# Query and key strips of an attention stage brought from 16 and 17 rows to 32

## The chip, the cores and the metric

The kernel runs on one core of a Trainium2 chip. The metric is the device time of one execution, in microseconds (us), lower is better. The engines are called as the profile calls them: PE is the matrix engine (TensorE), PEld its weight loads, DVE the vector engine, ACT the scalar engine, POOL GpSimd, SP the engine that only issues transfers here.

## The reference

The whole program is a chain of six blocks on an image batch of shape (8, 64, 32, 32): twelve layers of a state space model, a convolution block with attention, the image attention that is changed here, a graph attention with experts, a slice attention and a block of 16 experts. All is float32. The block that the change touches is this, per image (T = 1024 tokens, 64 channels, 4 heads of 16):

```python
Wh = (h @ W).reshape(B, T, 4, 16).transpose(0, 2, 1, 3)
scores = jnp.einsum('bhtd,bhsd->bhts', Wh, Wh) * 0.25
attention = softmax(leaky_relu(scores, negative_slope=0.2), axis=-1)
h_prime = jnp.einsum('bhts,bhsd->bhtd', attention, Wh)
```

Query and key are the same tensor. `h` is the layer-normed stream, and `h_prime` is added to it.

## The kernel before

The stages of the program run one after the other, each in a block of its own with its own semaphores. The stage in question is `graph_attn_stage` (L962). It works on 16 sets, one for each pair of heads of each of 8 images. A set has 16 slots: the 1024 query tokens in two halves of 512, times 8 blocks of 128 keys. The engines' queues are made from one list of slots, from -32 to 260, and each engine takes the slots in that order. A set's scores come in slots 0 to 15 of it; what prepares a set is spread over the slots of the sets before.

The identity leaky_relu(s) = max(s, 0.2 s) is used with exponentials: exp of the larger is the larger exp. So there are two branches, s and 0.2 s, each with its own strip of rows. `key` and `query` are tiles of 128 partitions that hold four strips of 32 partitions, for two heads times two branches (`head_rows`, L1047). In a strip, rows 0 to 15 are the head's 16 channels. Row 16 holds 1 in `key` and, in `query`, minus the query's largest possible exponent, so that a product over 17 rows gives the exponent already shifted. Rows 17 to 31 hold zeros: the weights `ws` that make the strips are padded with zero columns (an input prepared so), and ACT's bias `K_UNIT` is 1 on row 16 of each strip alone.

In one slot:

- `scores` (L1078): PE makes, for each of two heads, two products of 17 rows by 128 keys by 512 queries, one for each branch, into `g_ab` (one PSUM tile for each head). Each product is two instructions in the trace (float32). The products of head h wait until ACT has read head h's tile of the slot before (`exped`).
- `exps` (L1162): ACT takes the exponential of both branches of a head at once, 1024 columns, into `g_both`; `larger` (L1212): DVE takes the larger of the two branches for both heads.
- `sums` (L1093), every second slot: PE multiplies with the values, 128 rows by 32 columns, four at once into four column strips of `g_sum`; `keep_sum` copies it out at every fourth of these.
- `maxima` (L1107), for a coming set: PE multiplies 16 rows of `key` (128 of its tokens) with 16 rows of `key` (all 1024 tokens, in two strips) into `g_top`, of which DVE takes the row's maximum (L1224). A new product waits for the reading of the one before (`top_read`). It is placed after the slot's scores in PE's queue, so the next slot's scores stand behind it.
- `side` (L1121, and ACT's part L1177): single steps of a set, which share the PSUM tile `g_side`: `turn` and `values` once an image, `heads0` and `heads1` two sets ahead (PE makes half a tile, ACT writes `key` with the bias, then `query` with the scale and releases `g_side`), `rows` one set ahead, at slot 13 (the 16 columns of negated maxima are turned into rows; SP sends them to DRAM and back in four transfers to row 16 of each strip of `query`, and the set's first scores wait for `rows_in`), and `out` at slot 3 of the next set (the sums are turned back, DVE divides and adds).

POOL gathers for a later stage in the first slots of this one, and DVE goes on with that stage's search after its last slot.

Of the kernel before, what the change touches and what calls it, by code (L numbers as in the profile page):

```python
# [2 lines left out]
P = 128  # L3
B, C, H, W = 8, 64, 32, 32
L = H * W
# [953 lines left out]
HEADS2, HDIM2 = 4, 16  # L959


def graph_attn_stage(nc, w_strips, w_plain, consts, m_rows, tn_sb, t_sb, search):  # L962
# [9 lines left out]
    ALU, ACT, AX = mybir.AluOpType, mybir.ActivationFunctionType, mybir.AxisListType.X  # L972
# [41 lines left out]
    with ExitStack() as ctx:  # L1014
        def sb(name, shape, dt=fp32):
            return ctx.enter_context(nc.sbuf_tensor(name, shape, dt))
# [10 lines left out]
        tnT = [sb(f"g_tnT{k}", [C, L]) for k in range(2)]  # L1027
        val = [sb(f"g_val{k}", [P, PER, HEADS2, 32]) for k in range(2)]
        key, query = ([sb(f"g_{n}{k}", [P, L]) for k in range(3)] for n in ("key", "query"))
        both = [sb(f"g_both{k}", [P, 2, 2, HALF]) for k in range(2)]  # L1030
        E = [sb(f"g_E{k}", [P, 2, HALF]) for k in range(4)]
        oT = [sb(f"g_oT{k}", [P, HALF]) for k in range(2)]
# [11 lines left out]
        rows_out, rows_in = sem("g_rows_out"), sem("g_rows_in")  # L1044
        halves = [slice(0, HALF), slice(HALF, L)]

        def head_rows(h, branch, rows=HDIM2 + 1):  # L1047
            at = 32 * (2 * h + branch)
            return slice(at, at + rows)

        with nc.Block() as block:
            @block.sync
# [21 lines left out]
            @block.tensor  # L1074
            def _(pe):
                M = nc.tensor.matmul

                def scores(g):  # L1078

                    p, s = slot_of(g)  # L1080
                    half, j = divmod(s, PER)
                    if s == 0:
                        pe.wait_ge(rows_in, p * 64 + 64)
                    for h in range(2):
                        if g:
                            pe.wait_ge(exped, 2 * (g - 1) + h + 1)
                        for branch in range(2):
                            rows = head_rows(h, branch)
                            last = M(pair_ps[h][:, halves[branch]], key[p % 3][rows, j * P:(j + 1) * P],  # L1089
                                     query[p % 3][rows, halves[half]], start=True, stop=True)  # L1090
                        last.then_inc(scored, 1)

                def sums(r):  # L1093

                    pe.wait_ge(maxed, 2 * r + 2)
                    if r and r % 4 == 0:
                        pe.wait_ge(sum_kept, r // 4)
                    for g in (2 * r, 2 * r + 1):
                        p, s = slot_of(g)
                        j = s % PER  # L1100
                        for h in range(2):
                            at = 32 * (2 * (j % 2) + h)
                            last = M(sum_ps[at:at + 32, :], val[p // 2 % 2][:, j, p % 2 * 2 + h, :], E[g % 4][:, h, :],
                                     start=j < 2, stop=j >= PER - 2)
                    last.then_inc(summed, 1)

                def maxima(p, b):  # L1107

                    h, i = divmod(b, PER)
                    n = maxima_no[p, b]  # L1110
                    if b == 0:
                        pe.wait_ge(side_read, event_no["heads1", p] + 1)
                    if n:
                        pe.wait_ge(top_read, n)
                    for half in range(2):
                        rows = head_rows(h, half, HDIM2)
                        last = M(top_ps[:, halves[half]], key[p % 3][rows, i * P:(i + 1) * P], key[p % 3][rows, halves[half]],  # L1117
                                 start=True, stop=True)
                    last.then_inc(topped, 1)

                def side(kind, at):  # L1121

                    n = event_no[kind, at]
                    if n:
                        pe.wait_ge(side_read, n)
                    if kind.startswith("turn"):
                        first = at * PER + 4 * int(kind[-1])
                        for i in range(4):
                            last = M(side_ps[0:C, i * P:(i + 1) * P], tn_sb[:, first + i, :], con[:, K_ID:K_ID + P],
                                     start=True, stop=True)  # L1130
                    elif kind == "values":
                        for i in BLK:
                            last = M(side_ps[:, i * C:(i + 1) * C], tnT[at % 2][:, i * P:(i + 1) * P], wq[:, :], start=True, stop=True)
                    elif kind.startswith("heads"):
                        last = M(side_ps[:, :], ws[:, at % 2, :], tnT[at // 2 % 2][:, halves[int(kind[-1])]], start=True, stop=True)
                    elif kind == "rows":
                        pe.wait_ge(negated, at + 1)
                        last = M(side_ps[0:SLOTS, 0:P], negm[:, :], con[:, K_ID:K_ID + P], start=True, stop=True)
                    else:
                        pe.wait_ge(sum_kept, 2 * at + 2)  # L1140
                        for i in BLK:
                            last = M(side_ps[:, i * C:(i + 1) * C], oT[i // 4][:, i % 4 * P:(i % 4 + 1) * P], fold[:, :],
                                     start=True, stop=True)
                    last.then_inc(side_made, 1)

                pe.wait_ge(loaded, 48)
                pe.wait_ge(folded, 1)
                for g in slots:
                    if 0 <= g < ALL:
                        scores(g)  # L1150
                    if sum_at(g) is not None:
                        sums(sum_at(g))
                    if event_at(g):
                        side(*event_at(g))
                    if maxima_at(g):
                        maxima(*maxima_at(g))

            @block.scalar
            def _(act):
                A = nc.scalar.activation  # L1160

                def exps(g):  # L1162
                    for h in range(2):
                        act.wait_ge(scored, 2 * g + h + 1)
                        if g >= 2:
                            act.wait_ge(maxed, g - 1)
                        A(both[g % 2][:, h, :, :].rearrange("p a t -> p (a t)"), pair_ps[h][:, :], ACT.Exp).then_inc(exped, 1)  # L1167

                def keep_sum(r):

                    half = r // 4
                    act.wait_ge(summed, r + 1)
                    if half >= 2:
                        act.wait_ge(side_made, event_no["out", half // 2 - 1] + 1)
                    A(oT[half % 2][:, :], sum_ps[:, :], ACT.Copy).then_inc(sum_kept, 1)

                def side(kind, at):  # L1177
                    if kind == "out":
                        return
                    act.wait_ge(side_made, event_no[kind, at] + 1)  # L1180
                    if kind.startswith("turn"):
                        done = A(tnT[at % 2][:, halves[int(kind[-1])]], side_ps[0:C, :], ACT.Copy)
                    elif kind == "values":
                        act.wait_ge(ones_set, 2)
                        if at >= 2:
                            act.wait_ge(summed, (at - 1) * SLOTS)
                        done = A(val[at % 2][:, :, :, 0:HDIM2], side_ps[:, :].rearrange("p (i h d) -> p i h d", i=PER, h=HEADS2), ACT.Copy)
                    elif kind.startswith("heads"):
                        hs = halves[int(kind[-1])]
                        A(key[at % 3][:, hs], side_ps[:, :], ACT.Identity, bias=con[:, K_UNIT:K_UNIT + 1])  # L1190
                        done = A(query[at % 3][:, hs], side_ps[:, :], ACT.Copy, scale=con[:, K_UNIT + 1:K_UNIT + 2])
                    else:
                        if at:
                            act.wait_ge(rows_out, at * 16)
                        done = A(mT[:, :], side_ps[0:SLOTS, 0:P], ACT.Copy)
                    done.then_inc(side_read, 1)

                nc.scalar.preload_act_table_set("natural_log_exp_and_others")
                act.wait_ge(loaded, 48)
                for g in slots:  # L1200
                    if 0 <= g < ALL:
                        exps(g)
                    if sum_at(g) is not None and sum_at(g) % 4 == 3:
                        keep_sum(sum_at(g))
                    if event_at(g):
                        side(*event_at(g))
# [1701 lines left out]
```

## Time and profile before

| | |
|---|---|
| time, median of 3 runs | 12822.3 us (12805.16 to 12825.92) |
| profiled execution, own time | 12828.42 us |
| its span, first to last instruction | 12826.2 us |
| PE busy | 7784.8 us (61%) |
| DVE busy | 7413.5 us (58%) |
| POOL busy | 7085.3 us (55%) |
| ACT busy | 4851.3 us (38%) |
| mean granted TensorE clock | 0.746 of full speed |

The busy times are sums over stages that have different limits; the stage of the change is 12% of the span, from 7052 us to 8535 us. The granted clock is 1.00 for 2.4 GHz and 0.50 for 1.2 GHz, and a value between the two for a stretch is a mixture of both levels. The profiled execution was 6.1 us longer than the median of the runs, and 2.2 us of its time lie outside its span.

### The profile page before, as it was taken

Reading aid. Unit: us, or ns where it says so; the run is one execution under the profiler, and the core shown is the slowest. Engines: PE = TensorE matmul, PEld = TensorE weight load, DVE = VectorE, ACT = ScalarE, POOL = GpSimd, SP = SyncE. Lnnn points to the kernel's source line nnn. Section 1 sums busy time; section 2 is a strip of 40 time slices with the busy share of each in tenths; the row PEclk is TensorE's granted clock in tenths of the full one; section 3 lists DMA queues with packets and bytes.
Section 4 is the critical chain, followed back from the end, with each engine's and each line's share of the span. In section 5 each row is a group of like instructions: output and inputs, shape, how many; then the busy total and the mean of one; then the engine's idle time right before and its main releaser. Section 6 shows DMA issues by size and latency. Waiting matters only on the chain. (4 is left out here: it accounts for less than half of the span.)

```text
span 12826.2 us, 85840 instructions
## 1 busy us (share of the span) xinstructions
PE 7784.8 (61%) x22295; PEld 3300.0 (26%) x22295; DVE 7413.5 (58%) x5674; ACT 4851.3 (38%) x5239; POOL 7085.3 (55%) x4572
## 2 busy tenths in 40 slices
PE   0288888888888888887787799970000000000469
PEld 0133333333333333332343233330000000000342
DVE  8599999999999999998222344431111111110424
ACT  0166666666666666664011244430111111110124
POOL 0088888888888888887100100006666666666017
PEclk8599999999999999999666555555555555555569
DMA  0155555555555555555000000003222222221012
GB/s 8 39 154 155 155 155 155 153 156 154 155 155 155 153 155 156 154 156 142 4 0 0 8 1 1 1 2 34 16 16 16 16 16 16 17 17 11 3 38 89
DMA packets 387922, 959.19 MB, mean 75 GB/s; under 512 B 124066, under 2 KB 159458, under 8 KB 385442
## 3 DMA queue, kind: packets, MB, share of 16 engines
q1 hardware_dynamic: 302786, 930.45, 26.5%
q0 software_dynamic: 75808, 26.27, 4.7%
q10 hardware_dynamic: 9216, 1.05, 0.1%
q8 instruction: 61, 1.00, 0.0%
q14 instruction: 51, 0.42, 0.0%
HBM read 905.13 MB, written 50.89 MB: 75 GB/s over the span
## 5 line engine op out<-in xcount | busy, mean ns | idle before, releaser
L502 POOL TENSOR_TENSOR hC<-h,Cb 128x1024 f32<-128x1024 f32 x1536 | 3611.6, 2359 | 935.8 <-DVE h L581 934.8
L581 DVE TENSOR_TENSOR_SCAN h<-dA,B_ps 128x1024 f32<-128x1024 f32 x1536 | 3512.4, 2287 | 68.1
L285 PE MATMUL y_ps<-hC,con 128*128 128x512 f32 x6144 | 2910.4, 595 | 92.9 <-DVE gz L587 56.9
L432 ACT ACTIVATE dA<-delta,negA 128x1024 f32<-128x1024 f32 x1536 | 1765.8, 1150 | 1831.8 <-DVE h L581 1831.2
L2357 POOL DMA_INDIRECT g_got<-scratch_node,g_idx x2048 | 1951.8, 953 | 898.9 <-issue 898.7
L573 DVE TENSOR_TENSOR B_ps<-dx,B_ps 128x1024 f32<-128x1024 f32 x1536 | 1855.2, 1208 | 94.7 <-PE B_ps L279 94.7
L2373 PE MATMUL g_ps_y<-g_wout,g_hid 128*128 128x64 f32 x512 | 126.0, 428 | 2544.8 <-ACT g_hid L2413 1496.5
L285 PEld LDWEIGHTS y_ps<-hC,con 128*128 128x128 f32 x6144 | 1136.8, 189 | 1128.3 <-issue 740.5
L279 PE MATMUL B_ps<-Bpart,sel 96*128 96x512 bf16 x3072 | 925.7, 383 | 675.1 <-DVE h L581 674.0
L2443 DVE TENSOR_TENSOR g_e<-g_tgt,g_got 128x128 f32<-128x128 f32 x64 | 27.1, 424 | 2057.7 <-DMA g_got<-scratch_node,g_idx 2057.7
L2397 ACT ACTIVATE g_w_ps<-g_w 128x128 f32<-128x128 f32 x64 | 18.0, 282 | 2237.0 <-issue 901.5
L1089 PE MATMUL g_ab<-g_query,g_key 17*128 17x512 f32 x2048 | 846.5, 1091 | 10.0 <-ACT g_both L1167 10.0
L2247 POOL MEMSET r_ad<- 128x4 f32 x1 | 0.1, 102 | 1524.9 <-POOLq L1295 1524.9
L2373 PEld LDWEIGHTS g_ps_y<-g_wout,g_hid 128*128 128x128 f32 x512 | 113.9, 327 | 2645.4 <-ACT g_hid L2413 1556.2
L1224 DVE TENSOR_REDUCE g_mrow<-g_top 128x1 f32<-128x1024 f32 x256 | 313.6, 1225 | 789.1 <-PE g_top L1117 720.1
L1167 ACT ACTIVATE g_both<-g_ab 128x1024 f32<-128x1024 f32 x512 | 508.8, 1023 | 672.6 <-PE g_ab L1089 672.6
L279 PEld LDWEIGHTS B_ps<-Bpart,sel 96*128 96x128 bf16 x3072 | 234.2, 98 | 1670.4 <-DVE h L581 1407.2
L1117 PE MATMUL g_top<-g_key 16*128 16x512 f32 x1024 | 514.2, 1101 | 62.2 <-issue 39.8
L1071 POOL MEMSET g_val<- 128x1024 f32 x2 | 1.8, 950 | 913.3 <-POOLq L931 913.3
L1544 POOL TENSOR_TENSOR eb_scaled<-eb_above,eb_share 64x1024 f32<-64x1024 f32 x128 | 301.6, 2356 | 125.1 <-PE eb_ps L1498 76.7
L1089 PEld LDWEIGHTS g_ab<-g_query,g_key 17*128 17x128 f32 x2048 | 286.9, 312 | 287.5 <-issue 154.3
L1217 DVE TENSOR_TENSOR g_E<-g_both 128x1024 f32<-128x1024 f32 x256 | 311.3, 1216 | 51.6 <-ACT g_both L1167 51.4
(477 smaller groups left out, 10931.7 us busy)
## 6 DMA issues: line engine op xcount, KB each, us to landing
Cb<-scratch_c_rows SPq DMA_DIRECT2D x3072, 256.0 KB, 3.9
g_got<-scratch_node,g_idx POOLq DMA_INDIRECT x2048
eb_share<-scratch_gate_rows SPq DMA_DIRECT2D x128, 256.0 KB, 3.5
scratch_edge<-g_out SPq DMA_DIRECT2D x64, 384.0 KB
par<-in_ssm SPq DMA_DIRECT2D x48, 395.5 KB, 4.8
scratch_c_rows<-Crow SPq DMA_DIRECT2D x96, 128.0 KB, 3.7
scratch_place<-s_zero SPq DMA_DIRECT2D x4, 1024.0 KB, 8.6
g_tgt<-scratch_place SPq DMA_DIRECT2D x1, 4096.0 KB
```

The lines of the kernel that those rows point to most:

```text
L279: last = nc.tensor.matmul(B_ps[k % 2][:, hs], sel[:, n, :], Bpart[d][:, hs], start=True, stop=True)
L285: last = nc.tensor.matmul(y_ps[:, hs], con[:, K_ID:K_ID + P], hC[k % DEEP][:, hs], start=(k == 0), stop=(k == STEPS - 1))
L432: A(dA[k % DEEP][:, :], delta[d][:, :], ACT.Exp, scale=negA[:, n:n + 1]).then_inc(decay_ready, 1)
L502: G.tensor_tensor(hC[k % DEEP][:, :], hst[k % DEEP][:, :], Cb[k % DEEP][:, :], ALU.mult).then_inc(prod_ready, 1)
L573: V.tensor_tensor(B_ps[k % 2][:, :], dx[dir_of(k)[0]][:, :], B_ps[k % 2][:, :], ALU.mult).then_inc(dbu_ready, 1)
L581: V.tensor_tensor_scan(hst[k % DEEP][:, ::step], dA[k % DEEP][:, ::step], B_ps[k % 2][:, ::step], 0.0, ALU.mult, ALU.add).then_inc(scanned, 1)
L1089: last = M(pair_ps[h][:, halves[branch]], key[p % 3][rows, j * P:(j + 1) * P], query[p % 3][rows, halves[half]], start=True, stop=True)
L1117: last = M(top_ps[:, halves[half]], key[p % 3][rows, i * P:(i + 1) * P], key[p % 3][rows, halves[half]], start=True, stop=True)
L1167: A(both[g % 2][:, h, :, :].rearrange("p a t -> p (a t)"), pair_ps[h][:, :], ACT.Exp).then_inc(exped, 1)
L1217: V.tensor_tensor(E[g % 4][:, :, :], both[g % 2][:, :, 0, :], both[g % 2][:, :, 1, :], ALU.max).then_inc(maxed, 1)
L1224: V.reduce_max(mrow[:, b:b + 1], top_ps[:, :], AX).then_inc(top_read, 1)
L2357: nc.gpsimd.indirect_dma_start(out=got[k][:, j, :], out_offset=None, in_=node_tbl, in_offset=Off(ap=idx[k][:, j:j + 1], axis=0)).then_inc( ...
```

## The change

All products of the strips are taken over 32 rows, where the scores had 17 and the maxima 16. For the scores this adds rows that hold zeros on both sides. For the maxima it takes in row 16, which is 1 in `key`; so that it adds nothing, the moving operand is no longer `key` but `plain`, a new tile (two buffers) that ACT fills with the heads as they are, with row 16 zero. That is one more ACT instruction of 128x512 in each `heads` step, between the two that were there. Nothing else is moved.

```diff
+        plain = [sb(f"g_plain{k}", [P, L]) for k in range(2)]
...
-        def head_rows(h, branch, rows=HDIM2 + 1):
+        def head_rows(h, branch):
             at = 32 * (2 * h + branch)
-            return slice(at, at + rows)
+            return slice(at, at + 32)
...
-                        rows = head_rows(h, half, HDIM2)
-                        last = M(top_ps[:, halves[half]], key[p % 3][rows, i * P:(i + 1) * P], key[p % 3][rows, halves[half]],
+                        rows = head_rows(h, half)
+                        last = M(top_ps[:, halves[half]], key[p % 3][rows, i * P:(i + 1) * P], plain[p % 2][rows, halves[half]],
                                  start=True, stop=True)
...
                         A(key[at % 3][:, hs], side_ps[:, :], ACT.Identity, bias=con[:, K_UNIT:K_UNIT + 1])
+                        A(plain[at % 2][:, hs], side_ps[:, :], ACT.Copy)
                         done = A(query[at % 3][:, hs], side_ps[:, :], ACT.Copy, scale=con[:, K_UNIT + 1:K_UNIT + 2])
```

## Rows read from the trace of the kernel before

**Rows 1.** Busy time by stretch: us, busy of PE, PEld, DVE, ACT, POOL, then granted clock.
```profile
3000.00:3400.00 400.00, 337.68 (x881) 137.29 (x881) 391.64 (x232) 255.02 (x253) 331.65 (x146) 1.00 0.57 156
6617.00:6634.00 17.00, 17.00 (x21) 6.64 (x20) 6.53 (x6) 0.00 (x0) 0.00 (x0) 0.50 0.00 0
6678.20:6688.40 10.20, 10.20 (x25) 3.31 (x24) 0.00 (x0) 0.00 (x0) 0.00 (x0) 1.00 0.00 0
6800.00:7000.00 200.00, 180.43 (x366) 80.41 (x367) 49.79 (x47) 24.65 (x27) 0.00 (x0) 0.67 0.00 0
7177.00:8525.00 1348.00, 1328.27 (x4558) 463.49 (x4562) 599.92 (x568) 578.16 (x634) 0.00 (x0) 0.51 0.00 1
12500.00:12700.00 200.00, 200.00 (x828) 61.24 (x824) 95.52 (x140) 83.14 (x140) 158.90 (x69) 1.00 0.29 89
7203.60:7207.00 3.40, 3.40 (x20) 1.90 (x16) 0.07 (x1) 0.67 (x2) 0.00 (x0) 0.50 0.00 0
7207.00:7210.40 3.40, 3.40 (x27) 2.17 (x23) 2.36 (x2) 2.31 (x3) 0.00 (x0) 1.00 0.00 0
7210.40:7213.80 3.40, 3.40 (x15) 1.49 (x14) 0.86 (x1) 1.40 (x2) 0.00 (x0) 0.50 0.03 5
```

**Rows 2.** PE's instructions in order of time, in stretches of Rows 1: start, length.
```profile
6622.28 3.62 PE L751 MATMUL psA<-k_sb,q_sb 32*128 32x512 f32 x4
...
6672.57 16.60 PE L769 MATMUL psM<-E,vT 128*65 128x512 f32 x32 [2.41 <-ACT E L831]
...
12599.90 0.59 PE L1497 MATMUL eb_ps<-tnT_b,eb_w 64*128 64x512 f32 x1
12599.91 0.59 PE L1498 MATMUL eb_ps<-eb_scaled,eb_w 64*128 64x512 f32 x1
```

**Rows 3.** PE's instructions in order of time, around the stage's first rise of the clock.
```profile
7202.90 1.94 PE L1103 MATMUL g_sum<-g_E,g_val 128*32 128x512 f32 x8
7204.77 1.97 PE L1129 MATMUL g_side<-g_con,tn_a 128*64 128x128 f32 x8
...
7207.36 1.45 PE L1089 MATMUL g_ab<-g_query,g_key 17*128 17x512 f32 x6
7208.74 2.15 PE L1133 MATMUL g_side<-g_w,g_tnT 64*128 64x64 f32 x16
```

**Rows 4.** PE's instructions in order of time, two slots of the stage at clock 0.50.
```profile
7438.86 1.94 PE L1103 MATMUL g_sum<-g_E,g_val 128*32 128x512 f32 x8
...
7440.75 1.22 PE L1089 MATMUL g_ab<-g_query,g_key 17*128 17x512 f32 x2
...
7441.76 2.74 PE L1089 MATMUL g_ab<-g_query,g_key 17*128 17x512 f32 x6
...
7446.00 2.62 PE L1089 MATMUL g_ab<-g_query,g_key 17*128 17x512 f32 x8
7448.55 1.94 PE L1103 MATMUL g_sum<-g_E,g_val 128*32 128x512 f32 x8
```

**Rows 5.** Groups of the stretch 7177 to 8525: busy, mean ns, idle before and its end.
```profile
L1167 ACT ACTIVATE g_both<-g_ab 128x1024 f32<-128x1024 f32 x511 | 507.8, 1023 | 672.6 <-PE g_ab L1089 672.6
L1217 DVE TENSOR_TENSOR g_E<-g_both 128x1024 f32<-128x1024 f32 x255 | 310.1, 1216 | 49.6 <-ACT g_both L1167 49.5
L1224 DVE TENSOR_REDUCE g_mrow<-g_top 128x1 f32<-128x1024 f32 x238 | 291.5, 1225 | 695.0 <-PE g_top L1117 694.8
```

**Rows 6.** All engines in order of time, the last slots, which hold no maxima.
```profile
8486.82 2.09 PE L1089 MATMUL g_ab<-g_query,g_key 17*128 17x512 f32 x8
...
8494.81 2.09 PE L1089 MATMUL g_ab<-g_query,g_key 17*128 17x512 f32 x8
```

**Rows 7.** The same view of the start, and of one set's maxima on their way.
```profile
7072.43 0.69 ACT L1190 ACTIVATE g_key<-g_side,g_con 128x512 f32<-128x512 f32 x1 [2.16 <-issue]
7073.01 0.68 ACT L1191 ACTIVATE g_query<-g_side,g_con 128x512 f32<-128x512 f32 x1
...
7423.14 1.10 SPq L1064 DMA_DIRECT2D g_query<-scratch_m_rows  x4
```

## The prediction, made before the changed kernel was run

> **What bounds the kernel now.** I read busy time by stretch first. The stage's main part, 7177 to 8525 us, is 1348.0 us long; PE is busy in 1328.3 us of it, DVE in 600, ACT in 578, POOL in nothing [rows 1]. The groups say the same from the other side: ACT's exponentials stood idle 672.6 us for PE's scores, DVE's maxima 694.8 us for PE's products, and what was waited for the other way round is small [rows 5]. So PE sets the pace, 1348.0 / 256 = 5.27 us a slot.
>
> The same rows hold the peculiar thing: PE is 98.5% busy and its granted clock is 0.51, that is 1.2 GHz almost throughout. A busy PE has either level in this trace, and what differs is how many of the array's 128 rows the instructions fill:
> - one strip of 32 rows at a time (L751), PE 100% busy: clock 0.50 [rows 1, 2];
> - 128 rows (L769), PE 100% busy: 1.00 [rows 1, 2];
> - two strips of 64 rows side by side (L1497 and L1498 start 0.01 us apart): 1.00, for 200 us on end [rows 1, 2];
> - 84% busy, with products of 96 and 128 rows (the twelve layers): 1.00 [rows 1];
> - here: the stretch before the clock rose at 7207 held nothing but the sums and a turning of tokens, both of 128 rows; in the stretch after it came strips of 17 rows and products of 64 rows, and the clock went back to 0.50, with PE busy all the time [rows 1, 3]. The trace has five such rises in the stage.
>
> The turning has a unit matrix as its moving operand, nearly all zeros, and the clock rose after it all the same [rows 3]. So I read: what counts is rows taken part in, not their values, nor busy time.
>
> **The order of two slots, at the low clock.** From one sum to the next are 7448.55 - 7438.86 = 9.69 us [rows 4]. The sum takes 1.87 us of it (start to next start, 7438.86 to some 7440.73). The rest is nine passes: a pass over 512 columns is (2.74 - 0.20) / 3 = 0.85 us, six passes lie between 7440.75 and 7446.00 and three between 7446.00 and 7448.55 [rows 4]. Maxima of one pair of strips run beside scores of the other pair, so it comes to nine passes where one after the other would be twelve. 4.85 us a slot, then; the other 0.42 are the side steps.
>
> **What the change adds.** (a) Rows: 17 and 16 become 32. Does a pass get longer? The four passes of 32 rows at L751 took 3.62 us from first start to last end, 0.85 each and a tail of 0.2, as the 17-row passes do [rows 2, 4]. Cost nothing. The Trainium skill (TensorE: Matmul & The Clock Gate, LDWEIGHTS) says that weight loads go by columns and that the row count doesn't matter; by this too the sum stays as it is.
> (b) One ACT copy in each of 32 heads steps. ACT's second pass there starts 7073.01 - 7072.43 = 0.58 us after the first [rows 7]; I price the third alike. Four of them lie before the stage's first slots, two on the path of the first set (1.2 us). The other 28 lie among ACT's work, 28 x 0.58 = 16 us; ACT has 2.3 us of work a slot (578.2 / 256 [rows 1]), so at the old pace they hide in 3 us of idle time a slot. At a faster pace some delay the next exponential: I charge half, 8 us. Bounds: nothing, and 32 x 0.68 = 22 us.
> (c) `g_side` is released 0.58 us later; the next side step is at least a slot away, and the next set's maxima wait for `heads1` only four slots on. Nothing. SP's row transfers are untouched: four issues of 1.10 us together make up its last part [rows 7]. The chain has three slots until the set's first scores, 15.8 us now and some 10 at the pace below; at an estimated 5 us, the issues four times over, it stays hidden. `plain` has two buffers, and its last reader is more than a set behind when it is written again, so no wait is added.
>
> **What the change gives.** The mean number of rows at work, at the old pace: scores 2048 passes x 17 rows x 0.85 us, maxima 960 x 16 x 0.85, the sums 128 rows for 256 passes x 0.85, over 1348 us, with some 7 from side steps: 22 + 10 + 21 + 7 = 60 of 128. With 32 rows: 41 + 19 + 21 + 7 = 88. A slot of both heads' scores at once fills the array as the two 64-row strips do [rows 2], and scores beside maxima of the other pair fill it too. So dense stretches come in nearly every slot and the clock should rise soon after the first scores. Once it is high, a pass takes (1.45 - 0.16) / 3 = 0.43 us [rows 3].
>
> How long is a slot at the high clock? From below, PE's own work: two slots are 9 x 0.43 + 0.17 (change to whole rows) + a sum of 1.02 = 5.06, so 2.53; the side steps' 0.42 shrink to 0.6 of it (a choice: a half if all were streams, more where weight loads set the time), 0.25: 2.8 us. ACT (2.3 + 0.1) and DVE (1.216 + 1.225 + some 0.1 [rows 5]) come to 2.4 and 2.5, so neither is beyond this. From above, the chain of waits: in the last slots, without maxima, two slots take 8494.81 - 8486.82 = 7.99 us, though PE has little to do: scores, exponential, scores, exponential, sum in a row by the queues' order [rows 6]. Three of its pieces are PE streams of 1.71 us that halve: 7.99 - 2.56 = 5.43. Two maxima that overlap nothing add 1.9, the side steps 0.5: 7.8 for two, 3.9 a slot. In the middle of the stage part of the maxima overlap scores, as in the nine passes above; I take the mean of the bounds, 3.35 us.
>
> How much of the stage is at the high clock? Then waits appear on PE, and 64-column steps whose time is weight loads, so it will fall now and again and stay low for a while. The stage before this one, which goes back and forth between strips of 32 rows and products of 128, had 0.67 as a mean, so a third of its time at the high level; the twelve layers have 1.00 with 84% busy [rows 1]. At the high pace the rows at work are still 88 x 5.27 / (2 x 3.35) = 69 of 128. That is nearer the layers than the stage before, whose low half is one strip of 32. I take 0.80 of the time; the bounds are 0.34 and 1.00 by these two rows, and with so many more rows I call 0.55 the likeliest case's lower end.
>
> **The sum.** Slots per us: 0.80 / 3.35 + 0.20 / 5.27 = 0.277; 256 slots take 925 us in place of 1348: -423. Copies +9. Net -414. The start (its maxima wait for DVE and for transfers) and the stages around it are unchanged. Against the profiled execution: 12828.4 - 414 = 12414, span 12412. That execution was 6.1 us over the median, so the runs should come to 12822.3 - 414 = 12408.
>
> **Rivals.**
> 1. The clock doesn't move, because a started strip already counts as 32 rows, or zeros don't count, or busy time is what counts. Then only the copies are left: 12822 + 1 = 12823. For it: I infer the rule from some ten stretches. Against: four strips of 17 rows come often here and the stage stayed at 0.51, where two strips of 64 held 1.00 [rows 1, 2]. The Trainium skill (TensorE: Matmul & The Clock Gate, Part 1) has the clock go by how busy the engine has been; by that rule PE at 98.5% would be at 1.00 before, and padding would change nothing. The rows differ from it: 0.51. 10%.
> 2. It rises but falls back at once, since at 2.4 GHz the same work leaves PE waiting: 0.30 of the time high. 0.30 / 3.35 + 0.70 / 5.27 = 0.222 a us, 1151 us, -197 + 9: 12634. This is about the lower bound of a third. For it: each of the five rises ended at once (one of them in [rows 1]). Against: those came with 17 rows. 7%.
> 3. Faster still, high throughout and better overlapped than I allow: 256 x 3.1 = 794, -554 + 9: 12277. 4%.
> 4. Slower: the clock stays low and the new ACT copy falls on the path twice, since exponentials and the release of `g_side` both come later. 2 x 0.68 x 32 = 44 us: 12866. It decides from 0.80 us a step (26 us in all). Against: ACT's 673 us of waiting for PE [rows 5]. 2%.
>
> **How the numbers follow.** The forecast has 77%: 12408. Its own range: at 3.35 us and always high, 256 x 3.35 = 858, gives 12341; 0.55 at 3.9 gives 0.55 / 3.9 + 0.45 / 5.27 = 0.226, 1131 us, 12614. The whole range, 12310 to 12640, takes in rival 2's middle and leaves out rivals 1 and 4 and most of 3, with a little of the tails. What a measurement of this kernel can tell from no change is 0.2%, 26 us. Faster: forecast, rivals 2 and 3, 88%. Same: rival 1, 10%. Slower: 2%.
>
> **What would show it.** In the changed profile, the granted clock of the stage should be near 0.9 (0.5 + 0.5 x 0.8) and a slot 3.6 us, with most scores' passes 0.43 us apart; ACT's idle time for scores should fall from 673 us to some 300. PE should no longer be busy nearly all the time. 32 more ACT instructions of 0.68 us. If the clock reads 0.51 the rows' theory is wrong; if it reads 0.9 and a slot is above 4 us, the chain of waits was underpriced; if SP's transfers end PE's waits at every 16th slot, (c) was.

## The result, and the profile after

The changed kernel takes 12299.68 us (median of 4 runs, 12287.58 to 12304.47) where the kernel before, now run more often, takes 12813.73 us. The ratio is 0.9598, 95% interval 0.9581 to 0.9614: 4.0% faster, some 514 us. I had forecast 12408 with a range from 12310 to 12640. The direction and the mechanism were right; the gain was a quarter larger than the 414 us of the forecast, and the time lies 10 us below the range. Of those 10 us the starting point has a part: I had counted from 12822.3 us for the kernel before, and its median is now 8.6 us lower.

The page of the changed kernel, part 2: 40 slices of the span, busy tenths of PE and granted clock in tenths.

```profile
PE   0188888888888888888688779920000000000569
...
PEclk8599999999999999999866689955555555555569
```

Counted from 0, the slices 23 to 25, where the stage lies, have a clock of 5 each before and of 8, 9 and 9 now. Busy time by stretch of the changed kernel, columns as in [rows 1]; the first row shown is the stage from its first exponential to its last, the other three are a stretch just before a fall of the clock, the one after it, and the one in which it has risen again:

```profile
7167.50:7996.20 828.70, 764.33 (x4550) 290.00 (x4548) 598.42 (x567) 569.23 (x663) 0.00 (x0) 0.98 0.01 1
...
7493.90:7496.50 2.60, 0.40 (x2) 0.00 (x0) 2.54 (x4) 1.94 (x2) 0.00 (x0) 1.00 0.00 0
7497.20:7500.60 3.40, 3.40 (x16) 1.48 (x14) 0.58 (x1) 1.19 (x2) 0.00 (x0) 0.50 0.00 0
7500.60:7504.00 3.40, 3.40 (x28) 1.51 (x26) 1.77 (x2) 2.05 (x3) 0.00 (x0) 1.00 0.00 0
```

(The dots stand for rows of other stretches.) Before, the stage had 1348.0 us [rows 1], some 3 of them ahead of its first exponential; it has become 516 us shorter, 1345.1 to 828.7 when both are counted from the first exponential. The medians differ by 514 us and the two profiled spans (12826.2 and 12294.8) by 531, so this stage holds nearly all of the gain. Of the other 15 us of the spans' difference 14 lie ahead of it, 8 before the convolution block's first product of queries and keys and 6 from there to the stage's first step, in code that the change doesn't touch; they are a difference between two executions. DVE and ACT are busy 598 and 569 us, in substance as before. PE does the same passes in 764 us of busy time in place of 1325. The granted clock is 0.98, where it was 0.51: 2.4 GHz in place of 1.2.

The groups of the stage in the changed kernel, columns as in [rows 5]:

```profile
L1168 ACT ACTIVATE g_both<-g_ab 128x1024 f32<-128x1024 f32 x512 | 496.8, 1023 | 246.3 <-PE g_ab L1090 245.6 <-DVE g_E L1219 0.7
L1090 PE MATMUL g_ab<-g_query,g_key 32*128 32x512 f32 x2040 | 464.5, 630 | 9.0 <-ACT g_both L1168 9.0
...
L1226 DVE TENSOR_REDUCE g_mrow<-g_top 128x1 f32<-128x1024 f32 x236 | 288.9, 1224 | 199.9 <-PE g_top L1118 191.6
L1118 PE MATMUL g_top<-g_plain,g_key 32*128 32x512 f32 x944 | 271.8, 652 | 41.9 <-DVE g_mrow L1226 41.9
```

ACT's idle time for scores fell from 672.6 to 245.6 us and DVE's for maxima from 694.8 to 191.6 [rows 5]. They are the same instructions with the same means, 1023 and some 1224 ns; what is gone is waiting for PE. PE's instructions in order of time, two slots of the changed kernel, against [rows 4]:

```profile
7415.52 1.07 PE L1104 MATMUL g_sum<-g_E,g_val 128*32 128x512 f32 x8
7416.52 0.70 PE L1118 MATMUL g_top<-g_plain,g_key 32*128 32x512 f32 x2
7416.53 0.70 PE L1090 MATMUL g_ab<-g_query,g_key 32*128 32x512 f32 x2
...
7417.06 1.44 PE L1090 MATMUL g_ab<-g_query,g_key 32*128 32x512 f32 x6
7419.06 1.13 PE L1118 MATMUL g_top<-g_plain,g_key 32*128 32x512 f32 x4 [0.56 <-DVE g_mrow L1226]
```

Three passes that took 2.74 us take 1.44, the sum 1.07 in place of 1.94. And something is new: an idle time of PE in brackets, in which it waits for DVE to have read the last maxima. Before, it came to 1.4 us in the whole stage; now it is 41.9.

### The profile page after: what moved, and what is told of

It is laid out like the page before. It is cut to its first block and busy times, and to the rows that moved or that the text cites. A ratio compares the mean times of both kernels' runs of the same rounds, so it can differ in the third digit from the quotient of the medians.

```text
span 12294.8 us, 85872 instructions
## 1 busy us (share of the span) xinstructions
PE 7209.1 (59%) x22295; PEld 3122.8 (25%) x22295; DVE 7412.1 (60%) x5674; ACT 4837.6 (39%) x5271; POOL 7077.4 (58%) x4572
## 5 line engine op out<-in xcount | busy, mean ns | idle before, releaser
L1168 ACT ACTIVATE g_both<-g_ab 128x1024 f32<-128x1024 f32 x512 | 496.8, 1023 | 246.3 <-PE g_ab L1090 245.6
L1226 DVE TENSOR_REDUCE g_mrow<-g_top 128x1 f32<-128x1024 f32 x256 | 313.4, 1224 | 299.1 <-PE g_top L1118 218.6
L1090 PE MATMUL g_ab<-g_query,g_key 32*128 32x512 f32 x2048 | 468.3, 631 | 9.0 <-ACT g_both L1168 9.0
L1118 PE MATMUL g_top<-g_plain,g_key 32*128 32x512 f32 x1024 | 313.3, 690 | 103.0 <-DVE g_mrow L1226 60.3
```

What stands on the lines that cost most here:

```text
L1226: V.reduce_max(mrow[:, b:b + 1], top_ps[:, :], AX).then_inc(top_read, 1)
```

## The experiments

Theory 1, that of the prediction: PE's granted clock follows the rows that its instructions take part in. The rivals: it follows busy time alone; only full strips count; values count; or the gain has another cause (the new operand). Each kernel ran against the kernel before on the same chip, and the ratios are to it. Clock and length of the stage are rows of the view by stretch, from its first exponential to the end of its last larger-of-two, in one trace of each kernel.

| kernel | ratio (95%) | median, us | stage, us | clock |
|---|---|---|---|---|
| kernel before | 1 | 12800 to 12814 | 1345.1 | 0.51 |
| changed kernel | 0.9598 (0.9581 to 0.9614) | 12299.7 | 828.7 | 0.98 |
| copies only | 1.0001 (0.9991 to 1.0010) | 12801.3 | 1332.2 | 0.51 |
| maxima on 32 rows | 0.9915 (0.9898 to 0.9931) | 12689.2 | 1188.6 | 0.60 |
| both on 24 rows | 0.9843 (0.9826 to 0.9859) | 12601.0 | 1157.5 | 0.64 |
| scores on 32 rows | 0.9665 (0.9649 to 0.9681) | 12371.9 | 934.0 | 0.84 |
| both on 28 rows | 0.9652 (0.9636 to 0.9668) | 12358.4 | 900.0 | 0.88 |
| ones in the padding | 0.9610 (0.9594 to 0.9626) | 12315.7 | 828.6 | 0.98 |
| copy twice | 0.9639 (0.9623 to 0.9655) | 12347.4 | 861.3 | 0.96 |
| maxima first | 0.9603 (0.9587 to 0.9619) | 12309.4 | 829.5 | 0.95 |
| turning later | 0.9608 (0.9590 to 0.9625) | 12301.5 | 828.2 | 0.97 |
| copies on POOL | 0.9620 (0.9603 to 0.9638) | 12312.6 | 833.7 | 0.96 |
| convolution strips too | 0.9478 (0.9462 to 0.9493) | 12150.7 | 828.3 | 0.98 |
| all together | 0.9459 (0.9442 to 0.9476) | 12110.0 | 805.2 | 0.98 |

### One part of the change alone

Only the copy and the new operand, rows as before:

```diff
+        plain = [sb(f"g_plain{k}", [P, L]) for k in range(2)]
...
-                        last = M(top_ps[:, halves[half]], key[p % 3][rows, i * P:(i + 1) * P], key[p % 3][rows, halves[half]],
+                        last = M(top_ps[:, halves[half]], key[p % 3][rows, i * P:(i + 1) * P], plain[p % 2][rows, halves[half]],
...
+                        A(plain[at % 2][:, hs], side_ps[:, :], ACT.Copy)
```

> Only the new ACT copy and the new moving operand of the maxima; scores stay at 17 rows, maxima at 16. Theory 1, the rows that PE's instructions take part in set its granted clock: the clock stays at 0.51 in the stage, the time is that of the kernel before plus 1 to 22 us (the copies), some 12815 to 12835. Rival, the new operand is what helped (key is no longer read as weights and as moving operand at once): the stage is short as in the changed kernel, some 12300.

The rival falls: ratio 1.0001, clock 0.51. The time, 12801.3 us, lies below the 12815 to 12835 that I had named, but the kernel before took 12800.4 us beside it. The copies cost nothing that can be measured at the low clock; ACT waits for PE 652 us there. The stage is 13 us shorter in this trace than in that of the kernel before: it holds some 38 us at the high clock where the other has 17. Such short rises come in both, and with one trace of each I read no effect from it.

Only the scores on 32 rows (`rows=32` as the default of `head_rows`, the maxima as before, no copy):

> Only the scores go to 32 rows, maxima stay at 16 rows of key, no copy. Mean rows at work at the old pace 79 of 128, against 60 before and 88 with both. Theory 1 (rows count as they are): the clock is high for most of the stage, over 0.85 as a mean, time 12300 to 12450. Rival, only a stretch whose strips are all full counts: the maxima, in nearly every slot, break it, clock below 0.65, time over 12600.

Only the maxima on 32 rows (with the copy, scores on 17):

> Only the maxima go to 32 rows, with the copy; scores stay at 17. Mean rows at work at the old pace 69 of 128. Theory 1: between the two kernels, the clock goes up and down, 0.55 to 0.85 as a mean, time 12450 to 12780. Rival (only full strips count): the clock stays at 0.51, time 12815 to 12835.

Both times came out within theory 1's numbers, 12371.9 and 12689.2 us, and so did the second clock, 0.60; the first, 0.84, was just below the 0.85 that was named. Full strips aren't needed everywhere for the clock to rise: with the maxima at 16 rows in nearly every slot the clock was 0.84, high for two thirds of the stage. The two parts give 3.35% and 0.85%, together 4.2%; measured together they give 4.0%.

### The same instructions with fewer rows

```diff
-            return slice(at, at + 32)
+            return slice(at, at + 24)
```

and the same with 28.

> Scores and maxima both on 24 rows, with the copy: the same instructions as in the changed kernel, fewer rows. Mean rows at work at the old pace 73 of 128. Theory 1: between the two kernels, nearer the changed one, clock 0.65 to 0.95 as a mean, time 12320 to 12650. Rival (only full strips count): 0.51 and 12815 to 12835. Rival (a strip counts once it has more than 16 rows, so that the scores were never the matter): as changed, 12300.

> Scores and maxima both on 28 rows, with the copy. Mean rows at work at the old pace 36 + 17 + 21 + 7 = 81 of 128, about the 79 that the kernel with only its scores on 32 rows has. If it is the rows at work that set the clock, however they come together, the two should be alike: clock of the stage 0.80 to 0.93, time 12330 to 12420. Rival, full strips are what matters (32 or nothing): like the 24-row kernel or below, clock under 0.65, time over 12600.

24 rows: 12601.0 us, within the range that was named, but nearer to the kernel before than to the changed one, where I had expected the opposite; the clock, 0.64, was just below what I had named. 28 rows: 12358.4 us at 0.88, beside 12371.9 us at 0.84 for the kernel whose scores alone have 32 rows. Counted as in the prediction, the first has 36 + 17 + 21 + 7 = 81 rows at work at the old pace and the second 41 + 10 + 21 + 7 = 79. Two different edits with nearly the same rows have nearly the same time. That is the strongest evidence for rows: PE's instructions have the same count, order and columns in all these kernels. What it doesn't separate is rows from rows times columns: every product whose rows were changed has 128 columns. Full columns aren't needed, at least: products of 128 rows and 65 columns had the clock at 1.00 [rows 1, 2]. The stage by stretch, one row from each kernel. Copies only:

```profile
7175.50:8507.70 1332.20, 1311.57 (x4550) 454.28 (x4548) 598.70 (x566) 592.24 (x663) 0.00 (x0) 0.51 0.00 1
```

Both on 24 rows:

```profile
7171.00:8328.50 1157.50, 1118.51 (x4552) 398.27 (x4550) 598.62 (x566) 583.08 (x663) 0.00 (x0) 0.64 0.00 1
```

Both on 28 rows:

```profile
7169.10:8069.10 900.00, 839.43 (x4550) 317.71 (x4548) 598.65 (x566) 570.27 (x663) 0.00 (x0) 0.88 0.00 1
```

In the first PE is busy 98.5% of the time and has the low clock; in the third it is busy 93% and has mostly the high one. So a high busy share isn't enough for the high clock, and a somewhat lower one doesn't prevent it. Busy time does matter where there is little of it: in the 40 slices above, the changed kernel's slices 27 to 36 have PE at 0 tenths and the clock at 5.

### What the padding holds

```diff
-    k[:, K_UNIT] = row % 32 == HDIM2
+    k[:, K_UNIT] = row % 32 >= HDIM2
```

> The changed kernel with rows 17 to 31 of each key strip holding 1 in place of 0 (the query rows there stay 0, so the products are the same). Theory 1 (rows taken part in, whatever they hold): same as the changed kernel, 12290 to 12310, clock of the stage 0.98. Rival, values matter to the clock or to the time: different from it by more than 0.3%.

Ratio 0.9610 against 0.9598, intervals overlapping (the median, 12315.7 us, is 6 us above what theory 1 named, and the ratios differ by 0.12%, less than the rival's 0.3%), the stage 828.6 us and the clock 0.98 to the digit. With zeros or ones in `key`'s padding rows it is the same. The other side, `query`'s rows, stayed zero in both, so data that are nonzero on both sides weren't tried.

### The price of the copy at the high clock

```diff
                         A(plain[at % 2][:, hs], side_ps[:, :], ACT.Copy)
+                        A(spare[at % 2][:, hs], side_ps[:, :], ACT.Copy)
```

> The changed kernel with a second ACT copy of the heads in each heads step, into a tile that nobody reads: prices the added copy at the high clock. By my prediction's term (half of 0.58 us on the path, 32 times) +9 us on the changed kernel, 12300 to 12315. Rival, the copies are on the path in full at the high clock: +19 us or more. Rival, hidden: 0.

By medians it takes 48 us more, so the +9 of theory 1 was wrong and the rival's +19 or more came true. The stage took 861.3 us, 32.6 more than the changed kernel's 828.7, at a clock of 0.96: more than the 16 us that 28 copies last, start to next start. The clock has a part in it. In the 15 sets from the first to the last of the sets' turned maxima (`g_mT`), which take 27.5 us more (815.7 and 788.2), the low clock lasts some 58 us where the changed kernel has 26. At 5.27 us a slot low and 3.19 high (worked out further down), by an estimate from these rows, those 32 us cost 13; what is left, 15, is about the full length of the 28 copies.

The other way round, 28 of the 32 copies on POOL (PE's wait for them is left out here):

```diff
+                        nc.gpsimd.tensor_scalar(plain[at % 2][:, hs], key[at % 3][:, hs], con[:, K_UNIT:K_UNIT + 1], None,
+                                                ALU.subtract).then_inc(plain_made, 1)
...
-                        A(plain[at % 2][:, hs], side_ps[:, :], ACT.Copy)
+                        if at < 2:
+                            A(plain[at % 2][:, hs], side_ps[:, :], ACT.Copy)
```

> The changed kernel with 28 of the 32 added copies taken from ACT and made on the idle POOL, from the key tile (minus the unit row). The doubled copy cost the full 0.58 us each on the path at the high clock and let the clock fall longer. By that, taking 28 away gives -16 us or a little more, 12270 to 12290. Rival, the first copy was hidden and only the second was not: 0. Rival, POOL and DVE get in each other's way or the maxima now wait for POOL: 0 to +20.

No gain: 12312.6 us, the stage 833.7. The 15 sets took 783.8 us where the changed kernel took 788.2 (before: 1281.9). That difference is small but can be read: three traces whose stage has the same instructions, those of the changed kernel, of the one with ones in the padding and of the one with the convolution strips below, have 788.2, 788.3 and 787.8. The last slots, with the clock at 0.75 where the changed kernel has 0.93, took 9.5 us longer and more than gave it back. So taking 28 first copies away is worth some 4 us in those 15 sets, and adding 28 second ones costs 27.5. The price isn't in proportion even without the clock's part, and whether POOL's 1562 ns for such a copy hides a part of the gain I can't tell apart.

### What makes the clock fall, and what a slot waits for

In the middle of the changed kernel's stage the clock falls five times (at 7285.6, 7497.2, 7603.0, 7708.8 and 7814.6 us), each time at the turning of the next image's tokens. PE has been idle for 2.23 us before it, waiting for DVE. There are six such waits, 13.4 us in all; the one at 7392 us was followed by no fall. Two more falls are in the last slots. The wait at 7392, by stretch:

```profile
7390.00:7394.00 4.00, 1.91 (x16) 1.35 (x18) 2.43 (x5) 2.44 (x3) 0.00 (x0) 1.00 0.00 0
7394.00:7398.00 4.00, 4.00 (x32) 1.70 (x28) 2.36 (x2) 2.53 (x3) 0.00 (x0) 1.00 0.01 4
```

The one before the fall at 7497, all engines in order of time (the dots leave out weight loads, the maxima's products and some steps of DVE and ACT):

```profile
7494.63 1.21 DVE L1219 TENSOR_TENSOR g_E<-g_both 128x1024 f32<-128x1024 f32 x1
7495.77 0.25 DVE L1248 RECIPROCAL g_rden<-g_side 128x16 f32<-128x16 f32 x1
7496.05 0.42 DVE L1249 TENSOR_TENSOR g_tmp<-g_side,g_rden 128x256 f32<-128x256 f32 x1
...
7496.53 1.36 PE L1130 MATMUL g_side<-g_con,tn_a 128*64 128x128 f32 x8 [2.23 <-DVE g_tmp L1249]
...
7497.84 1.22 PE L1090 MATMUL g_ab<-g_query,g_key 32*128 32x512 f32 x2
...
7498.85 1.06 PE L1090 MATMUL g_ab<-g_query,g_key 32*128 32x512 f32 x2
```

The turning needs `g_side`, which DVE reads for the set before; DVE has its larger-of-two first in its queue. The next passes, 1.06 us in place of 0.59, are at the low clock. One slot more between the two steps takes the wait away:

```diff
-        if s in (4, 5) and p % 2 == 0 and p // 2 + 1 < B:
-            return f"turn{s - 4}", p // 2 + 1
-        if s == 6 and p % 2 == 0 and p // 2 + 1 < B:
+        if s in (5, 6) and p % 2 == 0 and p // 2 + 1 < B:
+            return f"turn{s - 5}", p // 2 + 1
+        if s == 7 and p % 2 == 0 and p // 2 + 1 < B:
```

> The changed kernel with the turning of the next image's tokens and its values one slot later (slots 5, 6, 7 in place of 4, 5, 6). In the profile after, PE stands idle 2.2 us before each turning, for DVE's last step of the set before, and the clock falls right after each of the seven. If this idle time is what makes it fall: no fall but at the stage's ends, clock of the stage over 0.99, -10 to -25 us on the changed kernel (12275 to 12290). Rival, it is the sparse products of the turning and of the output that make it fall: seven falls as before, time within 10 us of the changed kernel or only the idle 7 x 2.2 = 15 us less.

By stretch, all of the stage but its last slots, and the last slots; first the kernel with the turning later, then the changed kernel:

```profile
7177.00:7940.00 763.00, 717.49 (x4328) 274.65 (x4326) 576.35 (x547) 532.29 (x625) 0.00 (x0) 1.00 0.01 1
7940.00:8006.00 66.00, 56.36 (x230) 15.94 (x224) 22.69 (x21) 35.95 (x38) 0.00 (x0) 0.66 0.00 1
```
```profile
7177.00:7940.00 763.00, 707.74 (x4262) 272.22 (x4256) 565.02 (x536) 522.38 (x615) 0.00 (x0) 0.99 0.01 1
7940.00:7996.00 56.00, 47.01 (x254) 14.04 (x250) 26.80 (x26) 39.87 (x43) 0.00 (x0) 0.94 0.00 1
```

Half of the expectation came true (it counts seven falls, where five of six waits had one). None of PE's waits for `g_tmp` and no fall is left before the last slots, so the falls came with the idle time, not with the steps: the turning is there, one slot later, and the output products are unchanged. The 15 sets take 772.8 us, -15.4. But the last slots, which have no maxima, run at a clock of 0.66 where the changed kernel had 0.94. The two lower rows begin at the same time, when this kernel was already 5 us further on; from the last turned maxima to the stage's end it takes 66.8 us in place of 51.8, 15 us more. The sum is nothing: 0.9608.

```diff
+                    if maxima_at(g):
+                        maxima(*maxima_at(g))
                     if sum_at(g) is not None:
                         sums(sum_at(g))
                     if event_at(g):
                         side(*event_at(g))
-                    if maxima_at(g):
-                        maxima(*maxima_at(g))
```

> The changed kernel with PE's maxima of a slot placed before its sums and side steps, not after them. If a slot at the high clock is set by DVE waiting for the maxima and PE waiting for DVE's reading (the profile after shows 219 us of DVE waiting for maxima and 60 us of PE for DVE), DVE gets its work earlier and a slot falls from 3.24 to some 3.0 us, time 12220 to 12280. If PE's own stream sets it, or the next slot's scores come no earlier, no change: 12290 to 12310.

No gain as a whole, 0.9603. The 15 sets took 779.2 us, 9 less than in the changed kernel, in spite of a clock that was low for longer: some 58 us of these sets in place of 26. By the estimate above that costs 13 us, so the new order was worth some 22, and the clock took more than half of it back. The falls are at other places here than the turning: the first four of them come right after PE has been idle 0.83 us for an exponential, in the slots behind a `heads` step. Whether that idle time brings them no run tests. The last slots took 6 us more.

### The same idea in the stage before

In the convolution block's attention, products of one strip of 32 rows go one after another [rows 2]. Here there is nothing to put beside them, so each image's queries were laid in a tile of 128 partitions with zeros in the other 96, the keys of both images in one with zeros in its last 64 partitions, and the product taken over 128 rows:

```diff
-        q_sb, k_sb = sb("q_sb", [Q_COLS, L]), sb("k_sb", [Q_COLS, L])
+        q_sb, k_sb = [sb(f"q_sb{k}", [P, L]) for k in range(2)], sb("k_sb", [P, L])
...
+                for t in (*q_sb, k_sb):
+                    nc.gpsimd.memset(t[:, :], 0.0).then_inc(zeroed, 1)
...
-                        qb, kb = q_sb[32 * b:32 * b + 32, :], k_sb[32 * b:32 * b + 32, :]
+                        qb, kb = q_sb[b], k_sb
...
-                    A(q_sb[:, :], psM[0:Q_COLS, :], ACT.Identity, bias=cw[0:Q_COLS, CV_BQ:CV_BQ + 1]).then_inc(act_done, 1)
+                    for b in IMAGES:
+                        rows = slice(32 * b, 32 * b + 32)
+                        last = A(q_sb[b][rows, :], psM[rows, :], ACT.Identity, bias=cw[rows, CV_BQ:CV_BQ + 1])
+                    last.then_inc(act_done, 1)
...
```

> The changed kernel, and in the stage before it (convolution block with attention) the same idea carried further: its products of one strip of 32 rows, PE 100% busy at clock 0.50, are taken over 128 rows, with zeros in all others (query of each image in a tile of its own, one more ACT pass an image pair). Theory 1: these 384 passes of 0.85 us go to 0.43 us, and the clock of that stage from 0.67 to over 0.85; -130 to -200 us, 12100 to 12170. Rival (only packing of strips side by side raises the clock, or zero rows on the moving side don't count as here both operands' other rows are almost all zeros): clock unchanged, time 12300 to 12310.

12150.7 us, ratio 0.9478 against 0.9598: 149 us less than the changed kernel by medians, within the expectation; the clock of the stretch, 0.84, is just below the 0.85 that was named. Most of that stage by stretch, in the changed kernel:

```profile
6160.00:6960.00 800.00, 712.41 (x1563) 333.91 (x1563) 197.53 (x194) 93.35 (x98) 0.00 (x0) 0.65 0.00 0
```

and in this one:

```profile
6160.00:6800.00 640.00, 549.11 (x1534) 288.03 (x1533) 193.21 (x191) 92.83 (x97) 0.00 (x0) 0.84 0.00 0
```

PE's instructions of this kernel in order of time, as the clock rises:

```profile
6404.29 3.78 PE L753 MATMUL psA<-k_sb,q_sb 128*128 128x512 f32 x4
6407.86 2.95 PE L753 MATMUL psB<-k_sb,q_sb 128*128 128x512 f32 x4
6410.65 1.88 PE L753 MATMUL psA<-k_sb,q_sb 128*128 128x512 f32 x4
```

The same work (197.5 and 193.2 us of DVE, 93.4 and 92.8 of ACT) in 640 us where it took 800. Four passes take 3.78 us at first, about as they did over 32 rows (3.62 [rows 2]), and then 1.88. 96 of the 128 rows add nothing but zeros to an image's product, and the clock rises with them all the same.

### All together

Turning later, maxima first, copies on POOL, and the convolution strips:

> All that seemed good together: the changed kernel with turning one slot later, maxima before sums in PE's queue, the copies on POOL and the convolution stage's strips on 128 rows. If the gains add (-150, -17, -16 and, with the clock no longer falling, -20 for the order of the maxima): some 12100, ratio to the kernel before 0.944. If they share one wait: 12130.

12110.0 us, ratio 0.9459 (0.9442 to 0.9476), 5.4% faster than the kernel before and the fastest of all. The stage is 805.2 us. Its 15 sets take 755.5 us, 33 less than in the changed kernel, near the sum of the three (4 + 15 + 9, and no clock falls among them).

## Why the prediction was right and where it was wrong

**Rows at work set the clock.** Right, with one thing not told apart: rows, or rows times columns. Ratios from 1.0001 to 0.9598 go with the number of rows in otherwise equal products, and two edits with nearly the same mean rows nearly meet. Rival 1, no change, had three forms: strips that count as full, zeros that don't, busy time. The 24- and 28-row kernels, the ones and the convolution strips, and the kernel with copies only are against them in turn. The Trainium skill's account (TensorE: Matmul & The Clock Gate, Part 1), a clock that goes by how busy the engine is, doesn't by itself describe these runs: PE 98.5% busy at 0.51, and 92% busy (764 of 829 us) at 0.98. The low clock of the slices in which PE has next to nothing to do agrees with it.

**A pass is no longer over more rows.** Right: 0.43 us at the high clock over 17 [rows 3], 32 and 128 rows, 0.85 at the low. Weight loads too: of 128 columns each, the median load of 32 rows took 184 ns in the changed kernel and that of 128 rows in the twelve layers 188 ns. The Trainium skill's rule (TensorE: Matmul & The Clock Gate, LDWEIGHTS) that loads go by columns, not rows, agrees.

**The copy: +1 and +8 us.** At the low clock it cost nothing that the runs can tell. At the high clock moving it to POOL gave back some 4 us in 15 sets, where I had charged 8, so the term was of the right size for one copy; the second one's 27.5 us show that it doesn't scale. The copy itself lasts 588 ns, not the 0.68 us of its neighbour.

**A slot at the high clock: the mean of 2.8 and 3.9, 3.35 us.** Measured: 796 us at the high level (0.96 of 828.7, from the clock of 0.98) hold all 256 slots less the 6 that 33 us at 5.27 hold, 3.19 us. The bounds held and the middle was 0.16 too long, 41 us in 256 slots. This slot has the copies in it, which I had charged apart. PE is busy 92% of the time, so the chain of waits overlaps better than I allowed.

**"I take 0.80 of the time": the step that failed.** It is the larger of two terms that were mis-sized; the slot above is the other. The share of the stage at the high clock was 0.96. With that and the forecast slot, 0.96 / 3.35 + 0.04 / 5.27 = 0.294 a us, 870 us in place of 925: 55 us. This and the slot's 41 are 96 of the 105 us by which the stage's 828.7 us and my 925 + 9 differ, and the other 9 are the copies, which the measured slot contains. Together they put the time below the range; neither would have alone: a share of 0.96 with 3.35 us gives 870 us and a time of 12353, and 0.80 with 3.19 us gives 887 us and 12370. I took 0.80 from two rows, the stage before at 0.67 and the twelve layers at 1.00 with 84% busy, and set it between the two, if nearer the layers. The first was the wrong neighbour and deserved no weight: its low half is one strip of 32 rows, as the prediction itself says. The layers' row was the one like this stage, with PE less than fully busy on nearly full rows. I had also thought that waits and sparse steps would bring falls; the experiment with the later turning shows that in the changed kernel's 15 sets only one wait, before the turning, did, and that the low clock lasted only some 26 us there. That the lower bound of the range stood so near rested on the slot: even always high, 3.35 us gave 12341, and rival 3 beyond it, 3.1 us a slot, had only 4%. That rival came nearest, with 12277.

**SP's transfers** (c) stayed hidden: in the whole stage they end one wait of PE's weight loads, 0.8 us long. The start was unchanged, 124 us from the stage's first turning to its first exponential in both kernels.

What stays open: how the last slots, where no maxima stand beside the scores, come by one clock or the other (0.94 and 0.66 in two kernels that are alike there); why a second copy costs so much more than the first, even without the clock's part; what makes the clock fall where the maxima stand first; whether columns count as rows do; and whether rows with nonzero data on both sides would differ.

## What to carry to other kernels

Look at the granted clock of a stage where PE is busy nearly all the time: if it is at half, count the rows of its instructions, for their busy time doesn't explain it. Filling strips of 16 or 17 rows to 32 with zeros, and lone strips to 128, cost no PE time here and halved nearly every pass in the one stage and many in the other, 4.0% and 1.2% of the whole; partly filled strips gave part of it. Once the clock is high, what is worth looking for is single waits that leave PE idle, and an order that is faster at the high clock can lose its gain by lowering it.

## What the runs showed of the hardware that was not expected

The clock goes up with rows that hold zeros (96 of 128 in the queries and 64 in the keys, in the convolution strips). Once high, it held through a stage in which PE was idle 8% of the time, but of six idle times of 2.23 us before the turning five were followed by a fall. Between 24 and 28 rows the mean clock goes from 0.64 to 0.88, much steeper than the rows: a mean between the levels is a mixture of both, and what the rows change is how much of the stage is high.
